# Attention's value and denominator products of a chunk joined into one run of eight, with other pieces in slots set for it

## What is computed

```python
x = x + _L0_xattn_ref(_layernorm(x), ctx_1024, ...)   # 16 heads of 8, 154 keys and 64 memory keys
x = x + _L0_ffn_ref(_layernorm(x), ...)               # 512 hidden, gelu
x = x + _L1_xattn_ref(_layernorm(x), ctx_1024, ...)   # rms norm of q and k, 154 keys
x = x + _L1_ffn_ref(_layernorm(x), ...)               # 4 experts of 512, top 2
x = x + _L2_xattn_ref(_layernorm(x), ctx_1024, ...)   # rotary q and k, 154 keys
x = x + _L2_ffn_ref(_layernorm(x), ...)               # 8 experts of 352 and a shared one
x = x + _L3_xattn_ref(_layernorm(x), ctx_1024, ...)   # one head of 128
x = x + _L3_ffn_ref(_layernorm(x), ...)
```

## Time and profile before

| | us |
|---|---|
| median of three runs | 964.61 (962.47 to 964.93) |
| the profiled execution | 964.95 |
| its span, first to last instruction | 963.2 |
| PE busy in the span | 890.3 |
| DVE, ACT, POOL busy | 574.8, 444.9, 275.6 |

### The profile page before, as it was taken

The page is one execution under the profiler, slowest core; times in us unless marked ns, Lnnn a source line. Parts: engine busy times, 40 slices in busy tenths (PEclk is TensorE's granted clock), DMA queues, the critical chain, the costliest instruction groups (busy, mean ns, idle before and its releaser), DMA issues. The chain is left out here.

```text
span 963.2 us, 15428 instructions
## 1 busy us (share of the span) xinstructions
PE 890.3 (92%) x5522; PEld 635.3 (66%) x5522; DVE 574.8 (60%) x1401; ACT 444.9 (46%) x799; POOL 275.6 (29%) x402
## 2 busy tenths in 40 slices
PE   3799999999999998999989899998999999999994
PEld 3555464655565536889877655545888888888783
DVE  2866758574866756454546477765536344454478
ACT  7265574757574654243322456755224232222350
POOL 6321407263766441011111145432001000021152
PEclk9999999998999999999999899999999999999997
DMA  5000000001020110000000210100000000000001
GB/s 159 7 2 15 1 17 1 15 2 37 2 56 11 71 37 24 1 1 1 1 1 1 81 36 26 53 25 14 2 1 1 1 1 1 2 1 1 1 1 44
DMA packets 27573, 18.10 MB, mean 19 GB/s; under 512 B 6221, under 2 KB 25770, under 8 KB 27370
## 3 DMA queue, kind: packets, MB, share of 16 engines
q1 hardware_dynamic: 27498, 17.12, 6.3%
HBM read 15.63 MB, written 1.05 MB: 17 GB/s over the span
## 5 line engine op out<-in xcount | busy, mean ns | idle before, releaser
L1377 DVE TENSOR_REDUCE mneg<-PS 128x2 f32<-128x308 f32 (+1 forms) x384 | 180.1, 515 | 107.2 <-PE PS L913 106.3
L1848 ACT ACTIVATE work<-PS 128x512 f32<-128x512 f32 (+2 forms) x168 | 100.0, 597 | 249.0 <-PE PS L1104 235.3
L1546 DVE TENSOR_TENSOR work<-PS,work 128x512 f32<-128x512 f32 (+2 forms) x168 | 114.8, 685 | 166.3 <-PE PS L1104 122.6
L1825 ACT ACTIVATE work<-PS 124x512 f32<-124x512 f32 (+1 forms) x272 | 157.1, 601 | 89.3 <-PE PS L1039 88.2
L1118 PEld LDWEIGHTS PS<-down_w,work 128*128 128x128 f32 (+2 forms) x1344 | 157.9, 191 | 5.7 <-DVE work L1546 1.3
L1118 PE MATMUL PS<-down_w,work 128*128 128x128 f32 (+2 forms) x1344 | 158.5, 275 | 1.0 <-DVE work L1546 1.0
L1102 PE MATMUL PS<-xh_sb,arena 128*128 128x512 f32 (+2 forms) x336 | 138.0, 411 | 8.8 <-DVE work L1546 8.7
L1104 PE MATMUL PS<-xh_sb,arena 128*128 128x512 f32 (+2 forms) x336 | 132.7, 395 | 0.0
L1103 PE MATMUL PS<-xl_sb,arena 128*128 128x512 f32 (+2 forms) x336 | 132.1, 393 | 0.0
L1926 POOL TENSOR_SCALAR rstd<-bn_mv 128x4 f32<-128x4 f32 x32 | 7.6, 238 | 423.1 <-DVE bn_mv L1275 423.0
L913 PEld LDWEIGHTS PS<-kb_sb,qxt_sb 97*128 97x128 f32 x256 | 44.0, 190 | 61.6 <-DVE mneg L1377 28.7
(11 more groups left out here) (217 smaller groups left out, 1248.5 us busy)
## 6 DMA issues: line engine op xcount, KB each, us to landing
ctx_rep<-in_ctxT SPq DMA_DIRECT2D x12, 308.0 KB, 3.3
stage<-in_w SPq DMA_DIRECT2D x8, 256.0 KB, 3.9
stage<-in_wg SPq DMA_DIRECT2D x8, 176.0 KB, 2.5
stage<-in_wu SPq DMA_DIRECT2D x8, 176.0 KB, 2.4
x_res<-in_x SPq DMA_DIRECT2D x4, 256.0 KB, 5.4
down_w<-in_w SPq DMA_DIRECT2D x1, 1024.0 KB
down_w<-in_wd SPq DMA_DIRECT2D x8, 128.0 KB
out<-x_res SPq DMA_DIRECT2D x4, 256.0 KB, 2.3
```

Of the source, the lines that this page charges most:

```text
L1377: dve.tensor_reduce(mneg[:, a % 2, t, h0:h0 + 2], PS[:, bank_of["mx", a, m], 0:2 * (KT0 if layer == 0 else KC)].rearrange("p (h n) -> p h ...
L1546: dve.tensor_tensor(HH[0:rows, e % 2, j, :], PS[0:rows, 2 * (n % 2) + 1, :], SS[0:rows, n % 2, :], ALU.mult).then_inc(*sig["h"].mark((i, n)))
L1825: act.activation(p_tile(i, n)[0:rows, :], PS[0:rows, n % 2, :], ACT.Exp, scale=SCALE).then_inc(*sig["p"].mark((i, n)))
L1848: act.activation(SS[0:rows, n % 2, :], PS[0:rows, bank, :], ACT.Silu).then_inc(*sig["act"].mark((i, n)))
```

## The change

In `values` the denominator products move from slot 4c + 7 to slot 4c + 5, right behind the value products of the same chunk, so that eight matmuls (sixteen instructions) follow each other. No instruction is added or removed. The tables `SLOTS` and `SLOTS0` get new slots for some pieces: in each row, layer norms (`ln`), key copies (`kb`), parts of the query (`q1` to `qlow`) and key chains (`kproj` to `klow`), value blocks (`v`), and in one row the second transposition of maxima (`mt`). The diff shows all rows that change.

```diff
 SLOTS = (
     {"vs": 2, "rden": (3, 3, 3, 3), "on": 1, "finish": 6, "ln": (0, 1, 2, 3), "norm": 3, "kt": 0, "kb": (0, 0, 1, 1), "qxt": (1, 2, 4, 5),
-     "max": (3, 27), "mt": (1, 29), "v": (29, 30), "xt": 7, "q": 11, "q1": 9, "q2": 13, "q3": 10, "q4": 14, "qsplit": 15, "qlow": 16, "kproj": 13,
-     "k1": 10, "k2": 12, "k3": 15, "ksplit": 28, "klow": 29, "w": 4},
+     "max": (3, 27), "mt": (1, 29), "v": (29, 30), "xt": 7, "q": 11, "q1": 9, "q2": 13, "q3": 7, "q4": 11, "qsplit": 12, "qlow": 13, "kproj": 13,
+     "k1": 10, "k2": 12, "k3": 15, "ksplit": 26, "klow": 27, "w": 4},
     {"vs": 2, "rden": (3, 3, 3, 3), "on": 1, "finish": 6, "ln": (0, 1, 2, 3), "norm": 3, "kt": 0, "kb": (0, 0, 1, 1), "qxt": (1, 2, 4, 5),
-     "max": (3, 27), "mt": (1, 29), "v": (29, 30), "xt": 7, "q": 9, "q1": 7, "q2": 11, "q3": 8, "q4": 12, "qsplit": 13, "qlow": 14, "kproj": 13,
-     "k1": 10, "k2": 15, "k3": 18, "ksplit": 29, "klow": 30, "w": 4},
-    {"vs": 0, "rden": (0, 0, 0, 0), "on": 1, "finish": 6, "ln": (0, 1, 2, 3), "norm": 5, "kt": 0, "kb": (0, 1, 1, 2), "qxt": (2, 4, 5, 6),
-     "max": (5, 21), "mt": (1, 21), "v": (21, 22), "xt": 6, "q": 9, "q1": 8, "q2": 14, "q3": 11, "q4": 15, "qsplit": 16, "qlow": 18, "kproj": 12,
-     "k1": 10, "k2": 14, "k3": 17, "ksplit": 21, "klow": 20, "w": 6},
-    {"vs": 0, "rden": (0, 0, 0, 0), "on": 1, "finish": 6, "ln": (0, 1, 2, 3), "norm": 5, "kt": 0, "kb": (0, 0, 1, 3), "qxt": (2, 4, 5, 6),
-     "max": (5, 21), "mt": (1, 21), "v": (21, 22), "xt": 6, "q": 9, "q1": 8, "q2": 14, "q3": 11, "q4": 15, "qsplit": 16, "qlow": 20, "kproj": 12,
-     "k1": 10, "k2": 11, "k3": 14, "ksplit": 19, "klow": 18, "w": 6},
-    {"vs": 0, "rden": (0, 0, 0, 0), "on": 1, "finish": 6, "ln": (1, 2, 3, 4), "norm": 5, "kt": 0, "kb": (0, 0, 1, 1), "qxt": (3, 3, 5, 6),
-     "max": (5, 20), "mt": (1, 21), "v": (20, 21), "xt": 7, "q": 9, "q1": 8, "q2": 16, "q3": 13, "q4": 17, "qsplit": 18, "qlow": 19, "kproj": 12,
-     "k1": 10, "k2": 11, "k3": 14, "ksplit": 20, "klow": 19, "w": 7},
-    {"vs": 0, "rden": (0, 0, 0, 0), "on": 2, "finish": 6, "ln": (1, 2, 3, 4), "norm": 5, "kt": 0, "kb": (0, 0, 1, 1), "qxt": (3, 3, 4, 6),
-     "max": (5, 21), "mt": (1, 21), "v": (19, 22), "xt": 7, "q": 9, "q1": 8, "q2": 16, "q3": 13, "q4": 17, "qsplit": 18, "qlow": 19, "kproj": 12,
-     "k1": 10, "k2": 11, "k3": 14, "ksplit": 19, "klow": 18, "w": 8},
+     "max": (3, 27), "mt": (1, 29), "v": (29, 30), "xt": 7, "q": 9, "q1": 7, "q2": 11, "q3": 5, "q4": 9, "qsplit": 10, "qlow": 11, "kproj": 13,
+     "k1": 10, "k2": 15, "k3": 18, "ksplit": 27, "klow": 28, "w": 4},
+    {"vs": 0, "rden": (0, 0, 0, 0), "on": 1, "finish": 6, "ln": (0, 1, 1, 2), "norm": 5, "kt": 0, "kb": (0, 0, 0, 1), "qxt": (2, 4, 5, 6),
+     "max": (5, 21), "mt": (1, 23), "v": (19, 21), "xt": 6, "q": 9, "q1": 11, "q2": 14, "q3": 11, "q4": 16, "qsplit": 17, "qlow": 19, "kproj": 14,
+     "k1": 12, "k2": 16, "k3": 19, "ksplit": 21, "klow": 20, "w": 6},
+    {"vs": 0, "rden": (0, 0, 0, 0), "on": 1, "finish": 6, "ln": (0, 0, 1, 3), "norm": 5, "kt": 0, "kb": (0, 0, 1, 3), "qxt": (2, 4, 5, 6),
+     "max": (5, 21), "mt": (1, 21), "v": (19, 21), "xt": 6, "q": 9, "q1": 11, "q2": 14, "q3": 11, "q4": 16, "qsplit": 17, "qlow": 21, "kproj": 12,
+     "k1": 10, "k2": 11, "k3": 14, "ksplit": 17, "klow": 16, "w": 6},
+    {"vs": 0, "rden": (0, 0, 0, 0), "on": 1, "finish": 6, "ln": (0, 2, 3, 4), "norm": 5, "kt": 0, "kb": (1, 1, 2, 2), "qxt": (3, 3, 5, 6),
+     "max": (5, 20), "mt": (1, 21), "v": (20, 21), "xt": 7, "q": 9, "q1": 11, "q2": 16, "q3": 13, "q4": 18, "qsplit": 19, "qlow": 20, "kproj": 12,
+     "k1": 10, "k2": 11, "k3": 14, "ksplit": 18, "klow": 17, "w": 7},
+    {"vs": 0, "rden": (0, 0, 0, 0), "on": 2, "finish": 6, "ln": (1, 1, 2, 4), "norm": 5, "kt": 0, "kb": (0, 0, 1, 1), "qxt": (3, 3, 4, 6),
+     "max": (5, 21), "mt": (1, 21), "v": (19, 22), "xt": 7, "q": 9, "q1": 11, "q2": 16, "q3": 13, "q4": 18, "qsplit": 19, "qlow": 20, "kproj": 13,
+     "k1": 11, "k2": 12, "k3": 15, "ksplit": 18, "klow": 17, "w": 8},
 )
 SLOTS0 = (
...
-    {"ln": 6, "norm": 10, "rows": 13, "xt": 16, "after_xt": 17, "late": 20, "up0": (28, 28, 29, 29), "down0": (33, 34, 35, 36), "acc0": 36,
-     "ln2": 36, "norm2": 37, "xt2": 41, "q": 46, "q1": 45, "q2": 48, "q3": 48, "q4": 53, "qsplit": 53, "qlow": 54},
+    {"ln": 6, "norm": 10, "rows": 13, "xt": 16, "after_xt": 17, "late": 20, "up0": (28, 28, 29, 29), "down0": (32, 33, 34, 35), "acc0": 35,
+     "ln2": 35, "norm2": 36, "xt2": 40, "q": 45, "q1": 44, "q2": 47, "q3": 47, "q4": 52, "qsplit": 52, "qlow": 53},
...
-                if n % 4 == 3 and n >= 7:
-                    c = (n - 7) // 4
+                if n % 4 == 1 and n >= 5:
+                    c = (n - 5) // 4
                     mask = MV0 if layer == 0 else MV1
                     if c == 0 and 7 in taken:
                         pe.wait_ge(*taken[7])
```

## The result

The change makes the kernel slower: 982.9 us in the median of four runs (977.01 to 988.92) against 964.66 (962.47 to 964.93), ratio 1.0194 [1.0148, 1.0239]: slower clear of noise, by 1.5 to 2.4%. The forecast was 958.8, the range 948 to 970. The runs after the change fall into two pairs, 977.0 us with a mean granted clock of 0.972 and 988.8 with 0.959; the profiled one is of the first pair.

The account below looks back on a forecast made before the run. PE, busy 92% of the span and fullest in the attention items, was taken to bound the kernel. Forecast: 964.95 - 5.5 + 0.5 + 4.4 - 4.1 - 1.5 = 958.8 us, range 948 to 970 (the forecast's own 954 to 963).

Parts of the forecast that it names:

- layer 0, 28 chunks: Layer 0 attention: full joining gain 8.4 us, less 1.4 for exponential waits and 1.5 around gelu, net -5.5.
- layers 1 and 2, 24 windows: Six items with maxima, four windows each: about eight bare ones at +0.05, the other 16 at 0, net +0.5 us.
- the two items without maxima: Items before a feed-forward: four scores in a row wait for exponentials, 1.8 us in layer 1, 2.6 in layer 2, +4.4.
- six item ends: Last chunk's pair joins for 0.30 and denominators cover 0.38 of PE's 0.57 wait for the last maxima: 6 x 0.68, -4.1 us.
- moved slots: New table slots for queries, keys, value blocks and copies: -1.5 us in all, between -5 and +4.
- The price of the form: Going into 32-column products and out again costs 0.30 us; a joined run of sixteen instructions takes 1.89 us.
- The bare windows with eight maxima: Layers 1 and 2: the eighth maximum waits 0.35 us for VectorE's fourth reduction, net +0.05 instead of -0.30 a window.
- the third rival: The exit doesn't join: 0.09 belongs to a group's completions, a pair saves only 0.21, total 964.9 us; chance 0.10.
- Where a window has no piece beside the maxima: Layer 0: the third score after a run waits for the first exponential, about 14 windows at 0.1, 1.4 us.
- the banks' rival: VectorE's banks decide: PE waits on reductions in the 24 windows of layers 1 and 2, +0.5 each, 970.3 us; chance 0.18.
- The sign that I had named for a wrong prediction: PE's waits for reductions in the 24 windows of layers 1 and 2 sum to well over 10 us or nearly nothing.
- a rival with a chance of 0.10 and +6.8 us: The clock: new waits bring four more 3.4 us stretches at the lower granted clock, 965.6 us; chance 0.10.

Follow-up runs that it names:

- e1: Kernel before with only the code edit, values and denominators joined in every chunk, slot tables as before: 986.33 us, ratio 1.0242.
- e2: Kernel before with only the new slot tables, denominators still two slots behind the values: 961.52 us, ratio 0.9985.
- e11: As e1, but the maxima reductions of layers 1 and 2 take half the columns (output not exact): 969.88 us, ratio 1.0060.
- e5: Kernel before with each attention exponential over 256 of 512 columns (output not the attention's): 958.43 us, ratio 0.9938.
- e6: As e1, with the halved exponentials of e5 (output not the attention's): 973.19 us, ratio 1.0097.
- e3: As e1, but the two items without maxima (7 and 11) stay split: 978.31 us, ratio 1.0158.
- e9: As e1, with one full-width 128-column matmul between values and denominators, denominators not summed (output not the attention's): 1023.89 us, ratio 1.0619.
- e13: Kernel before with only 14 chunks joined, each item's fourth and layer 0's fifth, not in the items without maxima: 972.17 us, ratio 1.0085.
- e4: Changed kernel, with layer 0's two four-row feed-forward products on full 128-row operands (low-rank part not computed): 977.15 us, ratio 1.0144.
- e8: Kernel before with the denominators one score behind the values instead of two, nothing joined: 981.47 us, ratio 1.0162.
- e10: As e1, but split in the items without maxima, every fourth chunk and layer 0's fifth; 44 of 68 chunks joined: 968.60 us, ratio 1.0056.
- e14: Kernel before with new slots except old rows for items 3 and 5, and selected chunks joined, 15 by the rules: 965.71 us, ratio 1.0002.

## Why the prediction was wrong

Of the 24 us between forecast and result, about 13 are time at full clock and 11 are clock, if the forecast is taken with the 23 us that before loses. All at full clock, by the windows of the profiled runs of before, e1 (joining alone) and after; the forecast's terms are all of the joining but the last two:

| term | forecast | e1 | after |
|---|---|---|---|
| layer 0, 28 chunks | -5.5 | +1.8 | +0.4 |
| layers 1 and 2, 24 windows | +0.5 | +2.7 | +4.0 |
| the two items without maxima | +4.4 | +4.6 | +5.0 |
| six item ends | -4.1 | +0.9 | -0.8 |
| outside the attention items | 0 | +0.7 | -0.2 |
| moved slots, by e2 | -1.5 | | -0.1, in the terms above |
| clock, median of the runs | 0 | +9 | +11 |

**Right.** The price of the form: 1.85 us for a run, and where nothing waits a window is shorter by 0.28 to 0.40 (ten of 28 in layer 0, such as 5.18 to 4.83). The two items without maxima: 3.95 and 3.52 a window against 3.89 and 3.56, +4.6 in all against +4.4. That the sum fits so well is luck in part: the first two windows of layer 1's item came to +0.91 and -0.23 where +0.25 and +0.20 were forecast. The bare windows with eight maxima: 4.56 against 4.51, with VectorE's banks as what holds the later maxima, as e11 shows. That denominators wait for no bank 7, and that the exit joins; the third rival is out.

**Wrong: layer 0, by 7 us.** The step that failed is "Where a window has no piece beside the maxima", with full gain wherever it has one. I counted pieces as time that PE gives to ScalarE. But most of them come to ScalarE as well (a copy of 0.6 us, a split, a copy of the maxima), ahead of the exponential that PE needs next, and the denominator group was PE's work meanwhile. In these 28 windows PE's waits for exponentials went from 0.7 us in one wait to 5.6 in nine (e1). In the first three items 21 chunks together gained 0.7 us. The fourth lost 2.6: 1.95 in the window shown above and 0.82 in the one where ScalarE changes to gelu. I had 0.4 for that. Halved exponentials took only part of it away: between e5 and e6 the first three items gain 2.2, and the fourth still loses 1.5. That the pieces ahead of them make up the rest fits the rows above, but no run without those pieces shows it.

**Wrong: the item ends, by 5 us.** The 0.57 of the earlier trace rows was to be covered by the denominators. It stands unchanged in all four ends that have it (e1). Between the rows shown there lies one more, the last maximum; before, and then e1 at the same place (PE, then DVE):

```profile
339.22 0.41 PE L913 MATMUL PS<-kb_sb,qxt_sb 97*128 97x308 f32 x1
```
```profile
352.48 1.04 PE L1070 MATMUL PS<-work,mv_sb 124*32 124x512 f32 x8
353.45 0.41 PE L913 MATMUL PS<-kb_sb,qxt_sb 97*128 97x308 f32 x1
354.43 0.60 PE L923 MATMUL PS<-ident_sb,mneg 128*4 128x128 f32 x4 [0.57 <-DVE mneg L1377]
```
```profile
353.89 0.48 DVE L1377 TENSOR_REDUCE mneg<-PS 128x2 f32<-128x308 f32 x1 [1.41 <-PE PS L913]
```

The last maximum's product stands behind the run, joined or not, and its reduction is what the transposition waits for. What PE does ahead of that product can't cover the wait; VectorE had stood 1.41 by then. Three of six ends gained all the same (0.60, 0.33, 0.16) and three lost (0.83, 0.63, 0.55). In the losing ones PE waits longer for exponentials (1.5 instead of 0.8 us), newly for GpSimd's low part of the keys (0.72), and longer for exponentials and newly for the copy of the maxima (0.44).

**Mis-sized: the 24 windows.** +2.7 is +0.11 a window, within the bounds given (-0.30 to +0.39) but above the 0 that I took; three single windows of e1's layer 1 lie outside (+0.47, +0.58, +0.97). In the bare ones it was the banks' rival in kind, at +0.09 and not +0.50. The sign that I had named for a wrong prediction did not show: PE's waits for reductions in the 24 windows, those of over 0.15 us, sum to 3.5 us after and 3.2 before.

**Wrong: the clock.** I had it as a rival with a chance of 0.10 and +6.8 us. It costs 7 to 12 us more in e1, e3, e6, e9, e13 and after, which join the chunks beside the query preparation, but 3 in e11 and 6 in e4, which do so too, and none in the two kernels that bunch or join elsewhere (e8, e10). What failed is that the forecast has the clock at nothing, with only the low chance as a reason, and that the rival stops at four short stretches. The order of the work moves the clock, and by more than that. Which waits do it isn't shown.

**The slots.** -1.5 was near enough as a sum (e2: -0.5 at full clock by the medians, -0.1 by the windows), but for other reasons: -3.6 at the item ends of layers 0 and 1, +3.6 in the windows ahead of them, among them a new wait of 1.6 for GpSimd's low part of the keys. The working had seen that part come late, but had put the stand on ScalarE; it is PE's transposition of the keys that waits.

Two sums of the prediction are slightly off, without effect on its verdict: 0.4 in each of four items is 1.6 and not 1.5, and +0.40 a window gives 967.9 and not 967.6.

The largest single rival sum (banks, 970.3) fell short too: the rivals were taken one at a time, and layer 0, the item ends and the clock failed together. For layer 0 and the bare windows the cause is the cover that PE's second group had given to ScalarE and VectorE. The item ends are another matter, a wait that a group ahead of it never could cover, and the cause of the clock's share is open.

## What to carry to other kernels

A group of matmuls that stands in the middle of an alternation is also the time in which the other engine works off its queue; before it is moved, list what the other engine has queued at that point, pieces included, not only the operation that is waited for. Work covers a wait only if it stands between the product and the one that waits for its result, not ahead of both. Save the change of form only where a window has spare time for both engines, chunk by chunk, and measure the sum: windows read from different traces don't add up within 2 to 5 us. And compare span x granted clock beside the time, or a loss of clock hides what the edit did.

## What was not expected of the hardware

- Going from full-width to 32-column products and out again costs about 0.3 us: by the starts in the earlier trace rows, and by the ten windows of layer 0 that are 0.28 to 0.40 shorter with one such change less. With one small full matmul put between, e9 cost 0.56 a chunk. The Trainium skill ("TensorEngine Tiling (Array Packing)", "Key Properties") says that changing the tiling mode drains TensorE, without a price; the 0.3 fits, but that it is this drain no run here shows.
- The mean granted clock moves with the program's order: 67 runs of before lay at 0.974 to 0.981, those of e1, e3, e13 and the change, with the same instructions in another order, at 0.959 to 0.972. It isn't fixed by the order: after the change, one program had two values, 0.972 and 0.959, 12 us apart, and e14 ranged from 0.968 to 0.984.
- Long runs of narrow products can go without a lower clock (e10: 44 runs of sixteen, 22 us lost), and cutting the runs doesn't bring the clock back (e9: 35 us lost).
